# A graph layer's edge count: variance and scale behind the first count's one-hots, first normed tiles ahead of its logarithm, PSUM banks dealt anew

## What is computed

```python
def _layernorm(x, axis=-1, eps=1e-05):
    m = jnp.mean(x, axis=axis, keepdims=True)
    v = jnp.var(x, axis=axis, keepdims=True)
    return (x - m) / jnp.sqrt(v + eps)
...
q = ((x @ Wq[l].T + bq[l]) * scaling).reshape(n, H, DH)
k = (x @ Wk[l].T).reshape(n, H, DH)
v = (x @ Wv[l].T).reshape(n, H, DH)
scores = jnp.einsum('ehd,ehd->eh', q[tgt], k[srcidx])
m = jax.ops.segment_max(scores, tgt, num_segments=n)
p = jnp.exp(scores - m[tgt])
s = jax.ops.segment_sum(p, tgt, num_segments=n)
w = p / (s[tgt] + 1e-16)
agg = jax.ops.segment_sum(w[:, :, None] * v[srcidx], tgt, num_segments=n)
```

## Time and profile before

| | us |
|---|---|
| median of 3 runs | 1133.38 (1133.23 to 1137.29) |
| the profiled execution | 1137.21 |
| its span in the trace | 1135.4 |
| TensorE busy | 1040.7 (92%) |
| VectorE busy | 775.9 (68%) |
| ScalarE busy | 593.3 (52%) |
| GpSimd busy | 307.0 (27%) |

### The profile page before, as it was taken

The page is one execution under the profiler, slowest core; times in us unless marked ns, Lnnn a source line. Parts: engine busy times, 40 slices in busy tenths (PEclk is TensorE's granted clock), DMA queues, the critical chain, the costliest instruction groups (busy, mean ns, idle before and its releaser), DMA issues. The chain is left out here.

```text
span 1135.4 us, 18973 instructions
## 1 busy us (share of the span) xinstructions
PE 1040.7 (92%) x6636; PEld 865.6 (76%) x6636; DVE 775.9 (68%) x2429; ACT 593.3 (52%) x1108; POOL 307.0 (27%) x306
## 2 busy tenths in 40 slices
PE   4899899989899999999899999889999999989943
PEld 2677677787788888887799897768888888879831
DVE  6667565657577777777488710757777777738788
ACT  5452232346466666666335533656666666632444
POOL 1000000004344444443033100434444444303204
PEclk9899899999899999999999999999999999999976
DMA  6033301458412112113203414751211211322203
GB/s 143 23 129 101 114 23 45 100 145 196 98 38 60 37 39 62 38 39 111 102 1 120 97 40 103 165 136 38 60 38 37 60 37 37 110 85 59 39 1 91
DMA packets 51072, 85.10 MB, mean 75 GB/s; under 512 B 15518, under 2 KB 33818, under 8 KB 50724
## 3 DMA queue, kind: packets, MB, share of 16 engines
q1 hardware_dynamic: 50980, 83.92, 29.8%
HBM read 36.50 MB, written 21.61 MB: 51 GB/s over the span
## 5 line engine op out<-in xcount | busy, mean ns | idle before, releaser
L939 PE MATMUL banks<-k_stack,q_stack 128*125 128x416 f32 (+1 forms) x960 | 299.9, 399 | 10.9 <-DMA q_stack<-q_split 7.3
L1035 DVE CUSTOM_DVE_ANT_0 probs<-banks,scores_bias 125x416 f32<-125x416 f32 (+1 forms) x480 | 267.3, 582 | 60.5 <-PE banks L939 56.1
L919 POOL TENSOR_SCALAR probs<-probs,mass_inv 125x1250 f32<-125x1250 f32 x160 | 210.7, 1317 | 347.7 <-DVE mass_inv L1044 347.7
L953 PE MATMUL banks<-ident,probs 125*125 125x125 f32 x1600 | 260.4, 278 | 7.9 <-DVE probs_t L1026 4.7
L953 PEld LDWEIGHTS banks<-ident,probs 125*125 125x125 f32 x1600 | 242.9, 189 | 31.4 <-issue 22.0
L1005 ACT ACTIVATE probs<-probs,neg_peak 125x1250 f32<-125x1250 f32 x160 | 213.4, 1334 | 53.2 <-DVE neg_peak L1058 53.2
L994 ACT ACTIVATE probs_t<-banks 125x500 f32<-125x500 f32 x320 | 152.3, 477 | 118.9 <-PE banks L953 118.9
L968 PE MATMUL banks<-probs_t,v_pair 125*64 125x250 f32 x1600 | 186.2, 379 | 0.9 <-ACT probs_t L994 0.9
L939 PEld LDWEIGHTS banks<-k_stack,q_stack 128*125 128x125 f32 x960 | 148.0, 192 | 39.4 <-issue 17.0
L968 PEld LDWEIGHTS banks<-probs_t,v_pair 125*64 125x64 f32 x1600 | 107.5, 136 | 54.2 <-ACT probs_t L994 1.3
L1026 DVE COPY probs_t<-banks 125x500 f32<-125x500 f32 x160 | 108.1, 675 | 57.1 <-PE banks L953 57.1
(11 more groups left out here) (251 smaller groups left out, 1434.5 us busy)
## 6 DMA issues: line engine op xcount, KB each, us to landing
q_stack<-q_split SPq DMA_DIRECT2D x160, 125.0 KB, 2.3
scores_bias<-edge_bias SPq DMA_DIRECT2D x8, 1171.9 KB
edge_bias<-bias_row SPq DMA_DIRECT2D x10, 585.9 KB
k_stack<-k_lo SPq DMA_DIRECT2D x16, 312.5 KB, 4.3
resid<-residual SPq DMA_DIRECT2D x2, 2500.0 KB, 9.7
values<-v_stage SPq DMA_DIRECT2D x2, 2400.0 KB
residual<-t SPq DMA_DIRECT2D x4, 625.0 KB, 3.2
xs<-in_x SPq DMA_DIRECT2D x5, 480.0 KB
```

The source lines that it names most:

```text
L919: nc.gpsimd.tensor_scalar(probs[:, u % 4, :], probs[:, u % 4, :], mass_inv[:, u % 4:u % 4 + 1], 1.0, ALU.mult, ALU.mult).then_inc(att["pro ...
L939: mm = nc.tensor.matmul(pb[0:NT, t % 5, 0:sn], q_stack[:, n % 2, half, part, tile * NT:(tile + 1) * NT], k_stack[:, head * N + s0:head * N ...
L953: mm = nc.tensor.transpose(pb[0:NT, 5 + t % 2, j * NT:(j + 1) * NT], probs[:, u % 4, (j0 + j) * NT:(j0 + j + 1) * NT], ident[0:NT, 0:NT])
L1035: nc.vector.tensor_tensor_reduce(out=probs[:, slot % 4, s0:s0 + sn], in0=pb[0:NT, t % 5, 0:sn], in1=scores_bias[:, (n % GROUPS) * GROUP + ...
```

## The change

Four edits, all in the first stage. VectorE does `variance` after the second round of block 0's one-hots rather than after the first. ScalarE writes the normed tiles of pairs 0 and 1 before block 0's `logs` rather than after it. Job 11 goes to bank 6 rather than 4, and the cycle of banks from job 12 on is 4, 5, 7, 3, 6 rather than 5, 6, 7, 3, 4. The wait for `lower(4)` stands at job 12 rather than 11. No instruction is added or taken away.

```diff
-        BANKS = ((3, 3, 6, 7, 3, 4, 5, 3, 6, 7, 3, 4) + tuple((5, 6, 7, 3, 4)[i % 5] for i in range(len(JOBS[0]) - 11)),
+        BANKS = ((3, 3, 6, 7, 3, 4, 5, 3, 6, 7, 3, 6) + tuple((4, 5, 7, 3, 6)[i % 5] for i in range(len(JOBS[0]) - 11)),
...
-        LOWER_FIRST = {2: 1, 5: 2, 6: 2, 8: 3, 11: 4}
+        LOWER_FIRST = {2: 1, 5: 2, 6: 2, 8: 3, 12: 4}
...
                 act.wait_ge(consts, 12)
+                for jj in GAP_TURNS[0]:
+                    normed(jj)
                 for j in range(TILES):
                     logs(j)
                     for jj in GAP_REDUCES.get(j, ()):
                         lower(jj)
-                    if j == 0:
-                        for jj in GAP_TURNS[j]:
-                            normed(jj)
...
                     for i in range(STEPS):
                         step(j, first, before, 0, i)
-                    if j == 0:
-                        variance()
...
                     if j == 0:
+                        variance()
                         scale()
```

## The result

| | before | changed |
|---|---|---|
| median of 17 runs, us | 1135.88 | 1129.25 |
| lowest to highest | 1129.97 to 1140.51 | 1125.63 to 1133.74 |
| profiled execution, its span | 1137.21, 1135.4 | 1129.25, 1127.5 |

The ratio is 0.9945, with a 95% interval of 0.9931 to 0.9958: 6.2 us less (4.8 to 7.8); the medians lie 6.6 apart. Forecast were 9.9. The 1129.25 lie just outside the range of 1119.5 to 1129.0. The base that the prediction started from was 1133.38, the median of three runs; seventeen gave 1135.88, so 2.5 us of the miss in the absolute time are the base's. The rest, 3 to 4 us, is a gain that is smaller than forecast. In the profiled execution a gain of that size was made and given back, and this document is about where.

The account below looks back on a forecast made before the run. TensorE, busy 1040.7 of 1135.4 us, was taken as the bound, with gains only where it idles or runs at low clock: 5.1 (block 0) + 4.8 (banks) = 9.9, so 1133.4 - 9.9 = 1123.5 us; range 1119.5 to 1129.0.

Parts of the forecast that it names:

- Block 0: First stage: one-hot matmuls in one piece to 28.3, turns to 33; gain carried on from count 1 5.1 us (4.5 to 7.6).
- a sign of being wrong: Block 1 on VectorE: the forecast is wrong if it starts later than 30.2.
- The idle that moved: Before count 1: TensorE idles 4.0 us until `combine` ends at 37.2; the low clock behind it costs 2.5 (0 to 3.1).
- Gap 4 up to Wv's turns: Job 11 starts without waiting for `lower(4)`, 0.7 us idle remains, no low clock; turns at 119.8.
- the second part: Banks in gap 4: gain 4.8 us (2.3 to 4.8), one job of 2.3 under the wait plus 2.5 of low clock.
- the prediction's second sign: Gaps 1 and 4: the forecast is wrong if TensorE's clock falls in either.
- The clock falls elsewhere: Rival: a fall in gap 1 or 4, or a low stretch median runs lacked, costs 1.7 to 2.7 us; chance 0.27.
- The clock holds at count 1: Rival: full clock at block 1's count despite 4.0 us of idle; gain 12.4, time 1121.0; chance 0.12.
- The late transfer: Rival: one more TensorE wait for q_stack with low clock gives back 6.1 us, time 1129.6; chance 0.11.
- The table load: Before block 0's logarithm on ScalarE: a drain, not shown in the trace, would make the gain 0.5 us less.

Follow-up runs that it names:

- both halves: kernels with both `variance` behind block 0's second round and the first normed tiles ahead of the logarithm; with the banks of before 1129.32 us, ratio 0.9930.
- the late store: Changed kernel with SyncE's store of the shifted x's first six tiles issued behind the load of Wk: 1122.55 us, 0.9867; a second time 1121.68 us, 0.9871.
- both remedies: Changed kernel with the shifted x's store behind Wk's load and TensorE's read of block 5's `table` row before job 11: 1124.04 us, ratio 0.9873.
- banks alone: Kernel before with only the new banks and the wait for `lower(4)` at job 12: 1135.46 us, ratio 0.9980.
- before with the late store: Kernel before with only the store of the shifted x's first six tiles moved behind the load of Wk: 1134.76 us, ratio 0.9991.
- first part: Changed kernel with banks and job 11's wait as before, so only variance and normed tiles moved: 1129.32 us, 0.9930; a second time 1132.29 us, 0.9945.
- variance only: Kernel before with only `variance` moved behind the second round of block 0's one-hots: 1134.79 us, ratio 0.9975.
- normed tiles only: Kernel before with only the first normed tiles moved ahead of block 0's logarithm: 1133.85 us, ratio 0.9979.
- the early read: Changed kernel with TensorE's read of block 5's `table` row moved ahead of gap 4's jobs, before job 11: 1123.38 us, ratio 0.9883.

## Why the prediction was right and wrong

**Block 0: right.** Variance at 26.64 without a wait (26.4), VectorE's block 1 at 30.57 (30.2; by its letter a sign of being wrong, in size 0.4 us), `combine` at 36.05 (35.7), the normed tiles from 28.43 (28.0), the turns in 3.81 (4.0). Count 0's 54 matmuls came in one piece but ended at 29.15, not at 28.3: the first round was not done at 23.4 in this execution, and in the others with both halves the count's last matmul started between 28.2 and 29.6. That spread lies in the matmuls of the first microseconds: one of 512 columns takes 0.63 us to begin with and 0.38 later, and the change came between about 20 and 22.6 in the traces of before, of the changed kernel, of the late store and of both remedies. The windows show a granted clock of 1.00 all through, so they don't say why. The prediction took it as fixed, 6.48 us for the first 27, and took VectorE's chain as free of it. It isn't: where the first matmuls were slow longest, VectorE waited for free one-hots (0.46 us at 22.99 in the changed kernel, 0.92 with both remedies), its variance came at 26.64 and 27.12 rather than the 26.10 of the quickest, and count 1 was put off by as much (37.56 and 38.02 rather than 37.00). The idle of 3.92 stayed the same.

**The idle that moved: right.** 3.92 us (4.0) before count 1, ended by `combine`. Its low clock cost 1.30 + 11.57 against 0.73 + 9.82, 2.3 (2.5). Count 1 was done at 50.4 (50.2): a gain of 5.0 (5.1). How near that is to the forecast is in part luck. In the other executions with both halves its last matmul started between 49.05 and 50.98, and with the first stage's front as before it started at 55.27 in the profile that the prediction read, but at 54.10 and 54.16 in two others (banks alone, and before with the late store). The gain at this place is thus 3.1 to 6.2, by which executions are paired.

**Gap 4 up to Wv's turns: right, but for the size of one term.** Job 11 without a wait, idle 0.77 (0.7), no low clock, turns at 119.98 (119.8). Of the 4.8 forecast, 2.5 were the low clock behind job 11's wait, read from one execution. Six traces have that wait, 3.06 us in each, and their jobs 11 to 13 took 9.39 (before), 9.62, 9.43, 8.46, 8.45 and 6.93 us (first part twice, before with the late store, variance only, normed tiles only), where 6.9 is the full clock. The term was 2.5 to 2.7 in three, 1.5 in two and nothing in one. The prediction had this chance among its rivals, as median runs that lack a low stretch and so have it not to lose, but not in the bounds of the term.

**The step that failed** is the sentence that closes the second part: "From 140 us TensorE is busy 20.00 of 20, so nothing takes the gain back". Between the end of Wv's turns at 131.6 and 140 lay a wait that the trace of before already showed, 1.29 us with "issue" behind it, and it was in no term. The gain was carried past it as if it had a fixed place relative to TensorE. The length of the wait hangs on SyncE's stores, which follow block 4's bias row and so move with the first part only. The prediction had priced just such a read on VectorE (2.23 us, from a row) and did not ask how long TensorE's takes, or why it isn't always the same. Worked out in its own terms: 9.75 less 1.0 of idle and 3.3 of clock gives 5.4 when count 5 ends, and the measured 6.2 (4.8 to 7.8) holds that. By the letter the prediction's second sign, a fall of the clock in gap 4, came too, behind the turns rather than in front of them. The 5.4 are those of one execution: in the other trace of the changed kernel the read and the idle were the same (3.18 and 2.32), but the low clock cost 1.6, and count 5's last matmul started at 135.27, 8.1 before that of before. So the idle is shown as the cause of a loss of 2.6 to 4.3 us in single executions, and how much of the 3 to 4 us between the medians it is stays an estimate. The ratios speak for it: with the early read the changed kernel came to 0.9883, 13.3 us below before, of which 1.3 are idle that the kernel before already had. The 12.0 that are left (8.7 to 15.3, another chip) are not below the 9.9 forecast, so the removal of this one wait brought back what was missing.

**Rivals.** "The clock falls elsewhere" came nearest, with 1125.2 to 1126.2 from its base; it had the right kind of price and the wrong place. The place it named, gap 1 with its idle of 2.50, stayed at full clock in the changed kernel's profile (54.13, 2.05 for 16), but the same turns behind the same 2.49 took 3.5 to 3.8 in six of the fourteen traces (3.54 with the late store, 2.05 on its second run). The Trainium skill (TensorE: Matmul & The Clock Gate, Part 1) says that the gate isn't tied to the kernel's start and that the number of slow matmuls varies between runs of one kernel; the rows of block 0 and of gap 1 agree. "The clock holds at count 1" did not occur: the count's 54 matmuls took 11.46 or more in all ten traces in which 2.4 to 3.9 us of idle stood before `counting(1)`. The late transfer didn't come either: TensorE's wait for q_stack at 288.61 was 2.97 us, against 4.13. (The range's lower end, 12.4 and another 1.7 off 1133.4, is 1119.3 and not 1119.5; nothing hangs on it.)

**The table load.** No drain showed after it in the changed kernel either: 32.47 + 1.28, and the logarithm at 33.77. The 0.5 us that the prediction set aside for one stay out.

**What stays open.** By the ratios the late store is 8.9 us (0.9867 against 0.9945, other chips) and 7.6 us (0.9871 against 0.9938, one chip) below the changed kernel, where the first stage's traces show 3.9 (count 5's last matmul at 134.05 against 137.92) and 4.3 (131.01 against 135.27). The 1.3 us of idle that the kernel before already had are in these 3.9 and 4.3. Part of the gap on the one chip is the choice of execution: the profiled one of the changed kernel took 1124.94 us where its median is 1131.20 (of its eight executions two took 1123.5 to 1125 and the others 1129 to 1133), while that of the late store took its median, 1121.68. From the first matmul of the attention to the end, the thirteen changed or partly changed traces and the one of before lie between 878.4 and 883.2 us, with no order by kernel: 880.0 and 878.4 for the changed kernel, 878.6 and 879.5 with the late store, 882.6 before. One trace per kernel can't tell whether the late store also helps there.

## What to carry to other kernels

When a change slides work on one engine, list what on that engine is slowed by transfers, register reads included, and ask for each which transfers it will now stand among, since these are issued when another engine is done. A low clock that one execution shows is not a saving to count in full. An idle time in the old trace that is labelled only "issue" is a term of the sum, not background. And price a new idle of TensorE twice, once for itself and once for the clock behind it, which here cost up to three times the idle that was added.

## What the runs showed of the hardware

A register read of a few words from SBUF took 0.75 to 0.78 us with the transfer engines at rest, and 1.7 to 3.7 us on TensorE's queue with stores or loads under way (DMA share 0.95 from 120 to 124 in the changed kernel); on VectorE's queue it took 1.9 to 2.7 in the five traces with the late store. Where it left an idle in gap 4, TensorE's next matmul started about 1.4 us after the read ended. The share alone doesn't set it: at 12.5, with the loads of x under way (all transfer engines busy from 12.5 to 13.5 in the changed kernel), the same read took 0.96, and with the tail of a bias row's store under way 0.83. Nor does a slow read always cost: TensorE's at 78.9 in the kernel before took 2.53 behind long-queued q jobs and left 0.37 of idle, the one at 149.6 took 2.64 and left none. The Trainium skill (DMA: Bandwidth & Descriptors, Latency and other measured facts) gives a floor of about 0.6 us for such a read; the lowest row here is 0.75.

The low clock's cost depended on the execution more than on the idle time: the same 2.49 us in gap 1 cost nothing in the profiles of before and of the changed kernel and 1.4 to 1.7 in others, 2.32 us before count 5 cost 3.3 in one execution of the changed kernel and 1.6 in the other, and 3.06 before job 11 cost 1.5 to 2.7 in five traces and nothing in the sixth. So no length of idle can be named from these rows beyond which the clock falls.
